# First group of a two-layer conditioned sequence block: attention output taken by halves of sequences, second x scaled on ScalarE

## The reference

```python
def ada(x, t, gw, bw):                       # gamma, beta: one vector per sequence
    return (t @ gw.T)[:, None] * x * rsqrt(mean(x * x, -1) + 1e-6) + (t @ bw.T)[:, None]
h = ada(x, t, attn_gamma_w, attn_beta_w)
q, k, v = (split16(h @ W.T) for W in (W_q, W_k, W_v))          # 16 heads of 16
o = softmax(0.25 * q @ k.T) @ v                                 # within a sequence
x2 = x + (t @ attn_alpha_w.T)[:, None] * (merge(o) @ W_o.T)
h2 = ada(x2, t, ffn_gamma_w, ffn_beta_w)
x3 = x2 + (t @ ffn_alpha_w.T)[:, None] * (silu(h2 @ gate_w.T) * (h2 @ hidden_w.T) @ out_w.T + out_b)
y = (layernorm(x3) * w + b + tanh(t @ lin_w.T + lin_b)[:, None]) * w + b
```

## Time and profile before

| what | value |
|---|---|
| median of 3 runs | 495.25 us (495.18 to 495.62) |
| profiled execution, whole | 495.45 us |
| span of its trace | 493.6 us |
| PE busy | 476.3 us (97%), 4562 matmuls |
| DVE, POOL, ACT busy | 380.4, 272.8, 243.6 us |
| chain that ended last: PE, DVE, POOL, ACT | 88%, 5%, 3%, 1% |
| granted TensorE clock, mean over the span | 0.991 |

### The profile page before, as it was taken

The page is one execution under the profiler, slowest core; times in us unless marked ns, Lnnn a source line. Parts: engine busy times, 40 slices in busy tenths (PEclk is TensorE's granted clock), DMA queues, the critical chain, the costliest instruction groups (busy, mean ns, idle before and its releaser), DMA issues.

```text
span 493.6 us, 12003 instructions
## 1 busy us (share of the span) xinstructions
PE 476.3 (97%) x4562; PEld 404.3 (82%) x4562; DVE 380.4 (77%) x807; ACT 243.6 (49%) x372; POOL 272.8 (55%) x189
## 2 busy tenths in 40 slices
PE   7989999999999999999999999999999999999992
PEld 4768678898879987898888988798888988889991
DVE  5788777579876889778886788778896788684775
ACT  3684754346453655427462564537453375413341
POOL 3249455554568543854458445674538554626573
PEclk9899999999999999999999999999999999999997
DMA  8473076301923044400834027420644006400113
GB/s 199 146 200 117 1 201 144 69 2 23 233 68 87 1 135 121 129 20 0 224 66 113 0 75 180 101 48 0 172 94 138 0 17 156 129 2 5 40 48 82
DMA packets 36045, 44.24 MB, mean 90 GB/s; under 512 B 3120, under 2 KB 31024, under 8 KB 36016
## 3 DMA queue, kind: packets, MB, share of 16 engines
q1 hardware_dynamic: 36016, 43.85, 35.0%
HBM read 35.18 MB, written 4.47 MB: 80 GB/s over the span
## 4 chain that ended last, share of the span: by engine, by line
PE 88%; DVE 5%; POOL 3%; ACT 1%; DMA 1%; issue 1%; DVEq 0%
PE banks L724 31%; PE banks L743 17%; PE banks L489 8%; PE banks L595 5%; PE banks L524 5%; PE banks L672 5%; PE banks L764 4%; PE banks L636 3%; PE banks L641 3%; PE banks L780 2%; PE banks L583 2%; POOL gh L1727 1%; PE banks L560 1%; DVE smax L1294 1%; PE banks L695 1%; PE banks L795 1%
## 5 line engine op out<-in xcount | busy, mean ns | idle before, releaser
L724 PE MATMUL banks<-x2s,gh 128*128 128x512 f32 x672 | 167.5, 397 | 1.1 <-ACT x2s L1044 0.8
L724 PEld LDWEIGHTS banks<-x2s,gh 128*128 128x128 f32 x672 | 122.8, 188 | 28.4 <-issue 1.2
L1695 POOL TENSOR_TENSOR hs<-act_t,hs 128x512 fp32r<-128x512 f32 x56 | 72.0, 1286 | 129.4 <-ACT hs L1020 96.5
L743 PE MATMUL banks<-wout,hs 128*128 128x256 f32 x672 | 91.9, 286 | 0.4 <-POOL hs L1695 0.4
L743 PEld LDWEIGHTS banks<-wout,hs 128*128 128x128 f32 x672 | 85.4, 188 | 5.3 <-POOL hs L1695 0.7
L1020 ACT ACTIVATE hs<-act_t 128x512 fp32r<-128x512 f32 x56 | 35.3, 631 | 70.4 <-DVE act_t L1388 70.4
L1013 ACT ACTIVATE act_t<-banks 128x512 f32<-128x512 f32 x56 | 33.6, 600 | 67.3 <-PE banks L724 65.3
L1384 DVE SCALAR_TENSOR_TENSOR act_t<-act_t,banks 128x512 f32<-128x512 f32 x56 | 38.4, 686 | 29.9 <-ACT act_t L1013 29.3
L1311 DVE RECIPROCAL work_c<-banks 128x512 f32<-128x512 f32 x14 | 47.0, 3355 | 2.9 <-PE banks L636 2.9
L489 PE MATMUL banks<-xs,wqk 128*128 128x512 f32 x168 | 42.6, 404 | 0.7 <-ACT xs L949 0.7
L1388 DVE SCALAR_TENSOR_TENSOR act_t<-act_t,banks 128x512 f32<-128x512 f32 x56 | 38.5, 687 | 5.0 <-PE banks L724 0.9
(11 more groups left out here) (145 smaller groups left out, 773.4 us busy)
## 6 DMA issues: line engine op xcount, KB each, us to landing
xtok<-x_in SPq DMA_DIRECT2D x8, 512.0 KB, 5.2
work_c<-xn SPq DMA_DIRECT2D x16, 256.0 KB, 3.5
xres<-x_in SPq DMA_DIRECT2D x8, 512.0 KB, 7.2
row_aa<-rows_dram SPq DMA_DIRECT2D x16, 256.0 KB, 6.8
row_af<-rows_dram SPq DMA_DIRECT2D x16, 256.0 KB, 7.5
row_b<-rows_dram SPq DMA_DIRECT2D x16, 256.0 KB, 6.0
shift<-rows_dram SPq DMA_DIRECT2D x16, 256.0 KB, 6.0
y<-final SPq DMA_DIRECT2D x7, 512.0 KB, 3.2
```

The costliest lines, as they stand in the source:

```text
L724: last = mm(banks[:, base + part, :], gh[:, a, k, w:w + P], x2s[:, b, k, :], start=(n == 0), stop=(n == 5))
L743: last = mm(banks[:, t // 2, D * (t % 2):D * (t % 2) + D], hs[:, c % 2, b, P * t:P * t + P], wout[:, a, c, :], start=(c == 0 and a == b an ...
L1695: tt(hs[:, c % 2, 1, :], act_t[:, c % 2, :], hs[:, c % 2, 0, :].bitcast(F32), ALU.subtract)\
```

## The change

Six edits, all in the first group and in what of the second is prepared beside it; the loop over groups 2 to 6 and the last group are as before.

1. The four blocks of the first group are taken by part first (`FIRST_ORDER`: both head groups of sequences 0 to 3, then both of sequences 4 to 7). Reciprocals, products and cuts are of 128x256 each. `o_proj(0)` runs in two halves of 12 matmuls, each as soon as its own cuts are there, into banks 2 and 3; the residual and the squares of a half follow at once.
2. The transposed x of group 1 gets gamma and beta on ACT: 16 ACTIVATEs of 128x64 with scale and bias from the tables (`second_xn`), instead of four 128x512 instructions on DVE. Its high part is cut in two halves by ACT, its low part in two by POOL.
3. Weight cuts: chunks 4 and 5 get their high part from DVE (after `negate_max`), 2 and 3 from ACT earlier, 6 before the third exponential; POOL does all of 2 to 6 before the cuts of o. `finish_shift` moves behind `cut_lo(3)`, the inverse root for group 1 ahead of `q_out(0)`.
4. `second_kq` goes: group 1's k is projected as in other groups, q behind the transposes of x2n.
5. Fill-in matmuls: 3 inside `o_proj(0)` instead of 10 ahead of it, 4 ahead of the transposes of x2n instead of 5 behind them.
6. SP: loads 5 and 6, the store of the rows and the two `row_aa` loads stand ahead of `move_v(0)`.

```diff
-WARM_LOADS, WARM_LAST_MAX, WARM_MAX, WARM_OUTPUT, WARM_NORM = 3, 2, 5, 10, 5
+WARM_LOADS, WARM_LAST_MAX, WARM_MAX, WARM_OUTPUT, WARM_NORM = 3, 2, 5, 3, 4
...
-FIRST_O = (6, 1)
+FIRST_DEN, FIRST_O, FIRST_PROJ = (7, 0), (6, 1), 2
+FIRST_ORDER = tuple((h, part) for part in range(2) for h in range(2))
+CUT_ON_DVE = (4, 5)
...
             load_stage(4)
-            move_v(0)
             load_stage(5)
             load_stage(6)
             sp.wait_ge(setup_dve, SETUP_ALPHAS)
             sp.dma_start(rows_dram[:, 0:R_SHIFT, :], rows[:, 0:R_SHIFT, :]).then_inc(rows_stored, 16)
-            load_res(0)
             sp.wait_ge(rows_stored, 16)
             load_aa(0)
+            move_v(0)
+            load_res(0)
...
+                if rowed(g):
                     pe.wait_ge(k_ready, 4 * g + 4)
-                    project_qk(g, 0, 4, q_mm)
-                else:
+                elif not later(g):
                     pe.wait_ge(tables_ready, 3)
-                    project_qk(g, 0, 0, q_mm)
+                project_qk(g, 0, bank_of_q(g), q_mm)
             def v_proj(g):
...
-                    pe.wait_ge(p_ready, 4)
+                    pe.wait_ge(x2_steps, X2)
                 project_v(base, range(V_EARLY if later(g) else TT))
...
                 for j in range(J):
-                    last = mm(banks[32 * j:32 * j + 32, 0 if part else 7, quarter(part)], cst[:, C_BLK:C_BLK + 32],
-                              pt[:, 4 * part:4 * part + 4, j, :], start=True, stop=True)
+                    last = mm(banks[32 * j:32 * j + 32, FIRST_DEN[h], quarter(part)], cst[:, C_BLK:C_BLK + 32],
+                              pt[:, 4 * h:4 * h + 4, j, :], start=True, stop=True)
                 last.then_inc(den_mm if part else den_first, 1)
...
+                    for half, hi, lo in ((0, o_hi_first, o_lo_first), (1, o_hi, o_lo)):
+                        pe.wait_ge(hi, 2)
+                        tile(2 * half, range(4))
+                        tile(2 * half + 1, range(4))
+                        if not half:
+                            warm_up(wqk[:, 0, 0], WARM_OUTPUT, FIRST_PROJ + 1)
+                        pe.wait_ge(lo, 2)
+                        tile(2 * half, range(4, 6))
+                        tile(2 * half + 1, range(4, 6)).then_inc(op_mm, 1)
+                    return
                 pe.wait_ge(o_hi, 2 * g + 2)
...
             def head(g):
-                if rowed(g):
-                    k_proj(g)
-                else:
-                    second_kq()
+                k_proj(g)
                 v_proj(g)
+                if not rowed(g):
+                    pe.wait_ge(x2_stats, TT)
+                    warm_up(wqk[:, 0, 0], WARM_NORM, 0)
                 transpose_x2(g - 1)
                 if rowed(g):
                     ffn_out(g - 2, CH - 1)
-                    q_proj(g)
-                else:
-                    pe.wait_ge(k_ready, 4 * g + 4)
-                    warm_up(wqk[:, 0, 0], WARM_NORM, 5)
+                q_proj(g)
...
-                for part in range(2):
-                    first_sums(1, part)
-                    first_values(1, part)
+                first_sums(2)
+                first_values(2)
                 transpose_x(1)
-                warm_up(wqk[:, 0, 0], WARM_OUTPUT, 2)
+                first_sums(3)
+                first_values(3)
                 o_proj(0)
...
+            def second_xn(k, seqs):
+                act.wait_ge(xt_mm, 2)
+                for b in seqs:
+                    cols, seq = slice(L * b, L * b + L), SEQ + b
+                    done = xn_beta if k == KD - 1 and b == SEQ - 1 else xn_first
+                    nc.scalar.activation(xn[:, k, cols], banks[:, 4 + k, cols], ACT.Identity,
+                                         scale=tabs[:, SLOT[GA], k, seq:seq + 1],
+                                         bias=tabs[:, SLOT[BA], k, seq:seq + 1]).then_inc(done, 1)
+            def second_split(k):
+                act.wait_ge(xn_first, SEQ if k == 0 else KD * SEQ - 1)
+                if k:
+                    act.wait_ge(xn_beta, 1)
+                nc.scalar.activation(xs[:, 0, k], xn[:, k, :], ACT.Copy).then_inc((x0_hi, xs_hi)[k], 1)
             def x2_split(g):
...
                 nc.scalar.activation(cvec, cvec, ACT.Tanh).then_inc(setup_act, 1)
+                cut_hi(2)
                 pair_k(0, range(2))
+                cut_hi(3)
                 pair_q(0)
                 keep_v(0)
                 par_k()
                 act.wait_ge(zeroed, ZEROED)
                 place_v_kept(0)
-                cut_hi(2)
                 place_v_swapped(0)
-                exp(0, 0)
-                exp(0, 1)
-                cut_hi(3)
-                cut_hi(4)
-                exp(0, 2)
-                exp(0, 3)
-                o_split(0, 0)
-                cut_hi(5)
-                o_split(0, 1)
+                first_exp(0)
+                first_exp(1)
                 cut_hi(6)
+                first_exp(2)
+                first_exp(3)
+                first_o_split(0)
+                first_o_split(1)
+                second_xn(0, range(SEQ))
+                second_split(0)
+                second_xn(1, range(2))
+                first_o_split(2)
+                first_o_split(3)
+                second_xn(1, range(2, SEQ))
+                second_split(1)
                 cut_hi(7)
...
+                dve.wait_ge(ld_stage[n], 16)
+                V.tensor_copy(chunks[n][1], stage_view(n)).then_inc(stage_hi_dve, 1)
             def residual1(g):
...
@@ -1479,18 +1523,24 @@
                 setup_weights()
                 dve.wait_ge(stage_lo, 1)
                 stats_x(1, x2n)
+                dve.wait_ge(x_stats, XS * 2)
+                rsqrt_both(1)
                 q_out(0)
                 for n in range(4):
                     max_over_keys(0, n)
                 negate_max(0)
-                dve.wait_ge(x_stats, XS * 2)
-                rsqrt_both(1)
-                first_normalise(0)
-                first_normalise(1)
-                for k in range(KD):
-                    scale_shift_xn(1, k, x0_steps, 4 + 2 * k).then_inc(xn_beta if k else x0_steps, 1)
-                residual1(0)
-                stats_x2(0)
+                for n in CUT_ON_DVE:
+                    cut_hi(n)
+                for part in range(2):
+                    for h in range(2):
+                        first_reciprocal(2 * part + h)
+                    for h in range(2):
+                        first_product(2 * part + h)
+                dve.wait_ge(ld_aa, 32)
+                dve.wait_ge(ld_res, 16)
+                for half in range(2):
+                    residual1_half(0, half)
+                    stats_x2(0, range(2 * half, 2 * half + 2))
                 norm2(0)
                 gamma_x2(0)
...
+                cols = quarter(part)
+                tt(os_[:, 1, h, cols], work_c[:, 1, quarter(h)], os_[:, 0, h, cols].bitcast(F32), ALU.subtract)\
+                    .then_inc(o_lo if part else o_lo_first, 1)
+            def second_split():
+                for k in range(KD):
+                    pool.wait_ge((x0_hi, xs_hi)[k], 2)
+                    done = tt(xs[:, 1, k], xn[:, k, :], xs[:, 0, k].bitcast(F32), ALU.subtract)
+                    done.then_inc((x0_lo, xs_lo)[k], 1)
+                pool.wait_ge(x2n_scaled, TT)
             def beta_x2(g):
...
                 cut_lo(0)
                 pool.wait_ge(xs_lo, 1)
                 cut_lo(1)
-                pool.wait_ge(x_stats, XS * 2)
-                finish_shift()
-                cut_lo(2)
                 pool.wait_ge(norm1_steps, RS * 2)
                 tt(xtok[:, :, :], xtok[:, :, :], nt1[:, 1, 0, :].unsqueeze(2).to_broadcast([P, TT, D]),
                    ALU.mult).then_inc(xs_scaled, 1)
+                cut_lo(2)
                 cut_lo(3)
+                finish_shift()
                 cut_lo(4)
-                o_split(0, 0)
                 cut_lo(5)
-                o_split(0, 1)
                 cut_lo(6)
-                xs_split(1)
+                for m in range(4):
+                    first_o_split(m)
+                second_split()
             def main(g, ln=True):
                 f = g - 1
```

161 lines of the change are left out of this document (85 added, 76 removed).

## The result

The changed kernel took 499.19 us (median of 20 runs, 495.03 to 501.9) beside 494.4 for the kernel before (20 runs, 493.53 to 495.96): ratio 1.0085, 95% interval 1.0068 to 1.0101, so about 4.2 us slower (the medians themselves are 4.8 apart). I had said 495.4, range 494.0 to 496.9, most likely no change. The profiled execution took 501.9, the slowest of the 20; it shows the mechanism at its largest, and the medians show the usual amount.

The account below looks back on a forecast made before the run. PE's work between 42.6 and 53.4 us was taken to set the start of `gate_hidden`, which moves the end one to one. Ladder -0.65 plus exchange +0.85 gave +0.2: 495.65 profiled, 495.4 median, range 494.0 to 496.9.

Parts of the forecast that it names:

- v's exchange: SP's exchange, issued behind weight loads, store and `row_aa`, lands later and shifts the first exponential by 0.85 us (0.2 to 1.5).
- rival D: `row_aa` is taken strictly before the exchange, first exponential at 32.4 or later: +0.85 to +1.85 us, chance 0.22.
- outer bound: Largest shift of the first exponential by the late exchange that the prediction allowed: 3.1 us.
- far end: Case of `row_aa` issued together with the exchange: shift 4.1 - 0.6 = 3.5 us, called unlikely.
- rival E: TensorE's clock falls from 1.00 to 0.50 in new idle time of 42 to 48: +2.5 us, chance 0.06.
- `finish_shift` and the root for group 1 lie in idle time: nothing: Moving these two earlier in the first group was put at no cost.
- The cuts of weights: Moved cuts on DVE, ACT and POOL fit where those engines wait or are free: nothing, bounds 0 and +0.3.
- The ladder: Chain of engine steps ahead of group 0's `gate_hidden`: transposes and gamma of x2 earlier, gain 0.9 or 0.4, taken 0.65 us.
- The ACTIVATEs: Second x on ACT: 16 of 64 columns, spaced 0.30 us, bounds 0.27 and 0.46; DVE loses four instructions of 0.69.
- The wait ahead of k's low part: PE waits for POOL's low part of x, until 47.4 us, or 47.9 if POOL stood behind DVE.
- A locked square: DVE square excluded by POOL's cut of x: one adds 0.45 us; gain 0.3 if POOL won each time.
- q behind the transposes: Group 1's q, 2.8 us on PE, runs while x2s is prepared: costs nothing, up to 0.1.

Follow-up runs that it names:

- e6: Changed kernel with the exchange of v issued by ACT, in a queue of its own, instead of by SP; ratio 1.0125 to the kernel before.
- e5: Changed kernel with 17 more unread matmuls on PE between the second scores and the first denominators; 498.48 us, ratio 1.0074 to the kernel before.
- e4: Changed kernel with SP waiting for the exchange to land before issuing residual rows and the last two weight loads; ratio 1.0079 to the kernel before.
- e2: Kernel before with only SP's first group in the new order; 499.9 us, ratio 1.0129.
- e15: Kernel before with one edit, the inverse root of group 1 ahead of `q_out(0)` on DVE; 497.09 us, ratio 1.0058.
- e16: Kernel before with one edit, ACT's weight cuts 2 and 3 ahead of k and of q; ratio 1.0011.
- e3: Changed kernel with the exchange ahead of the `row_aa` loads, still behind both weight loads and the store; ratio 1.0017 to the kernel before.
- e8: e11 with q of group 1 projected right behind k, ahead of v and the transposes; 499.21 us, ratio 1.0101 to the kernel before.
- e7: e11 with gamma and beta of group 1's x again on DVE; 495.48 us, ratio 1.0015 to the kernel before.
- e11: e10 with ACT's weight cuts 2 and 3 moved back later, POOL's order following; ratio 1.0006 to the kernel before.
- e1: Changed kernel with SP's first group in the old order, exchange early; 494.72 us, ratio 1.0011 to the kernel before.
- e9: e1 with the inverse root of group 1 back behind the last maximum, ACT's cuts left early; ratio 1.0009 to the kernel before.
- e10: e1 with SP holding the last two weight loads until the output projection's first half is done; ratio 1.0009 to the kernel before.
- e12: e11 without the hold on the last two weight loads; ratio 1.0004 to the kernel before.
- e18: Changed kernel with old SP order, cuts 2, 3 and root late, cut 5 in DVE's gap and between POOL's o halves; 494.75 us, ratio 0.9999 to before.

## Why the prediction was wrong

- **The step that failed** is "**v's exchange**": "I take **0.85**, between 0.2 and 1.5". Its mechanism was named (rival D), its size was almost five times too small: the first exponential moved by 4.1 in the profile. That is beyond the prediction's outer bound (3.1) and its "far end" (3.5) as well; the price it gave rival D, +0.85 to +1.85, did not reach its own outer bound, which would be 3.1 - 0.65 = +2.45. The exchange landed at about 33.6, where I had 31.1. I had priced it from `row_b` behind `row_aa`, +4.1, and subtracted 1.7 to 2.0 for a `row_aa` issued 3.5 us ahead; it was issued 2.3 ahead, and the second half of the exchange took 4.8 longer to land than before (8.4 for 3.6), with no discount. In-order taking (rival D's argument) cannot be the whole of it, since a queue of its own (e6) did not free the exchange. And the 0.39 DMA share of 24 to 27, which I held against a delay, says nothing of one: in the changed kernel the share over the same stretch was 0.41 with `row_aa` in flight. The rule of the Trainium skill, "DMA: Bandwidth & Descriptors", "Queues, rings and completion order", gave a shift of 1.5 in the prediction, by way of the row of `row_b` and that discount. The shift was 4.1, and no run tests the rule alone.
- **The clock (rival E)** was put at 42 to 48, where it fell in no profile at all. It fell behind the empty stretch that the late exchange makes, and cost 2.2 us beside before, 2.4 beside e5. I gave the shift and the clock as separate cases; in three profiles (after, e4, e6) the one brought the other, in e2, with an empty stretch of 2.88 us, it did not.
- **"`finish_shift` and the root for group 1 lie in idle time: nothing"** was wrong as well, for the root: moved alone it costs 0.6% (e15). The idle time was that of one kind of run, and I had one profile. The cuts of weights, also at nothing, are not clear of nothing in the times (e16), but the profiles of the early kind show a price: the first of them waits 1.35 us for its load in e3, and k is placed 1.2 later.
- **The ladder was right**: gain 0.4 to 0.9, taken 0.65, measured 0.8 in the changed kernel's own profile (19.27 for 20.06). The ACTIVATEs took 413 ns each and were 0.294 us apart ((2.47 - 0.413) / 7) for 0.30. The estimate from the Trainium skill, "ScalarE: Activation LUTs", "What ACT_TABLE_LOAD costs", was 332 ns, above the measured spacing (and its 585 ns for the 554 of the earlier trace rows was 5 to 6% off, not within 5%). The wait ahead of k's low part was 0.36 for 0.35, ahead of k 0.56 for 0.75, ahead of half 1 1.09 for 1.65. A locked square was there (1.49 us in the profile of after), but that wait of 0.36 is the one of the higher value. q behind the transposes cost about 0.1, as taken, and ahead of them would have cost 2.6 (e8). What the prediction had wrong inside the ladder is whom to thank: its 16 ACTIVATEs bring nothing that a profile shows (e7).
- So why doesn't the changed kernel with the early exchange gain 0.8? In the late kind it does, in the one profile there is: e11's `gate_hidden` is at 56.13 for 56.95. In the early kind the early root and the early cuts of ACT delay the first exponential by 0.6 to 2.5 us in e1, e3, e7 to e10 and e12, most where the clock falls behind PE's waits; by e15 the root does this alone. With both late (e18), the weight cuts as placed there took back 0.4 of the ladder; whether another place would cost less is untested. Each of these is one profile beside another of its kind; that they add up to the medians of e1, e10, e11 and e12 is argued.

## What to carry to other kernels

A DMA that a whole chain waits for should be issued ahead of large loads: moving it behind a broadcast of 512 KB cost more than all that the compute part of the change could bring, and in the one trial here another queue was no way out. A wait on PE can be paid twice, once as itself and once at half the clock behind it: after waits of 3.1 to 5.9 us the clock fell and cost 1.1 to 2.4 us more (e6, after, e4), after 2.9 us (e2) it did not fall, so give both cases when weighing a gain. "Idle time" read from one profile must be looked for in a second one, since the start of this kernel runs in two kinds 1.4 us apart. And compare profiles from a point behind such differences (here the third denominators), since a distance that spans them credits their time to the wrong edit, as it would have in e7.

## What the runs showed of the hardware

- The same two 256 KB transfers landed in 2.9 to 4.0 us with `row_aa` behind them (before, e1, e3, e12 and the rest), in 5.3 to 8.6 with it issued 1.4 to 2.3 us ahead (after, e2, e4, e5), and in 8.8 to 10.6 from ACT's queue with `row_aa`, `xres` and `row_b` ahead (e6). `row_aa` itself landed 6.1 us after its issue (median, after).
- A DVE square of 0.42 us took 2.43 and 2.60 beside POOL cuts of 2.40 and 2.57: this agrees with the exclusion for the whole length of an instruction that the Trainium skill, "SBUF — State Buffer", "Who interferes with whom", gives for a DVE instruction with two SBUF inputs beside a GpSimd one that reads SBUF, and it is larger here than I had it in any term.
- Issuing the same two DMAs for group 0 took 2.77 us on ACT (e6) and 1.14 to 2.49 on SP (e7, e2).
- The granted clock over 14 to 18 us was 0.57 to 0.67 in seven profiles and 1.00 in twelve, with the first exponential 1.5 us apart (30.8 and 29.3) where nothing was moved ahead of it. The runs of the kernel before fall into two groups as well: beside e18, twelve took 493.9 to 494.6 us at mean clocks of 0.993 to 0.995 and five 495.4 to 497.0 at 0.990 to 0.991. Most are thus not like the profile that I predicted from.
